# A graph kernel stores its edge records in slot order and loads them into lanes one record at a time

## What is computed

```python
x = x + L0_gnn(layernorm(x), src, dst, ...)      # attention over incoming edges, then a dense layer
x = x + L0_ffn(layernorm(x), ...)                # eight experts, two per node
x = x + L1_gnn(layernorm(x), edge_attr_4, edge_attr_8, (src, dst), ...)
x = x + L1_ffn(layernorm(x), ...)                # two banks of eight experts
```

## Time and profile before

| | us |
|---|---|
| median of 3 runs | 1942.54 (1939.13 to 1943.98) |
| span of the profiled execution | 1941.4 |
| `front`, to the first load of `count_edges` | 322.5 |
| of it from the first to the last scatter's issue | 19.26 to 229.74 |
| `count_edges` | to about 403 |
| attention | to about 709 |
| dense layer, first experts, small network | to about 1272 |
| `messages` | to about 1672 |
| last stage | to 1941.4 |

### The profile page before, as it was taken

One profiled execution on the slowest core, in us unless ns is written; L12 is line 12 of the kernel. 1 busy time (PEld: TensorE's weight loads), 2 busy tenths in 40 slices (PEclk: granted clock), 3 DMA queues, 4 the chain that ended last, 5 costly groups with the idle time before them and its releaser, 6 DMA issues. The chain is left out here.

```text
span 1941.4 us, 31644 instructions
## 1 busy us (share of the span) xinstructions
PE 1611.2 (83%) x9860; PEld 1169.5 (60%) x9860; DVE 958.2 (49%) x1950; ACT 701.1 (36%) x1610; POOL 561.3 (29%) x638
## 2 busy tenths in 40 slices
PE   1132298889999999889999999946999999898994
PEld 0111153568888865555999999934555455654662
DVE  8200023967776657654000000065999999632233
ACT  0000032745555543345222221144555555441331
POOL 6777500020110012125000000044555555123133
PEclk6565598989999999889999999968999999998997
DMA  9600011010103030065766554075555555518985
GB/s 292 240 7 6 18 40 41 1 26 18 23 11 82 10 84 2 1 238 163 284 232 234 197 207 171 9 186 142 159 158 152 146 157 155 190 59 270 354 260 185
DMA packets 131143, 252.87 MB, mean 130 GB/s; under 512 B 35344, under 2 KB 52596, under 8 KB 126572
## 3 DMA queue, kind: packets, MB, share of 16 engines
q1 hardware_dynamic: 91692, 171.81, 26.4%
q0 software_dynamic: 39360, 79.86, 14.7%
HBM read 196.03 MB, written 55.52 MB: 130 GB/s over the span
## 5 line engine op out<-in xcount | busy, mean ns | idle before, releaser
L2065 PE MATMUL acc<-prod,ohy 128*64 128x256 f32 x1056 | 250.7, 387 | 13.7 <-issue 7.5
L2109 ACT ACTIVATE ohy<-oh,RECS 128x64 f32<-128x64 f32 x704 | 186.7, 336 | 160.3 <-PE acc L2065 128.2
L2065 PEld LDWEIGHTS acc<-prod,ohy 128*64 128x64 f32 x1056 | 138.9, 138 | 140.0 <-issue 71.5
L2042 POOL DMA_INDIRECT rows<-up_dram,idx x176 | 167.4, 951 | 151.9 <-DVE prod L2183 107.0
L417 PE MATMUL ps<-FT,Wqkv 128*128 128x512 f32 (+1 forms) x192 | 88.1, 591 | 114.3 <-issue 114.3
L2068 PE MATMUL acc<-prod,ohy 128*64 128x256 f32 x704 | 179.6, 397 | 0.0
L273 POOL DMA_INDIRECT rec_dram<-recs,pos x157 | 161.6, 1029 | 60.2 <-issue 48.9
L1819 DVE TENSOR_SCALAR FT<-y_ps,b2T 128x188 f32<-128x188 f32 x32 | 13.2, 414 | 323.3 <-PE y_ps L1768 323.3
L1756 PE MATMUL hid_ps<-FT,W 128*128 128x188 f32 x1024 | 167.7, 325 | 0.7 <-ACT FT L1793 0.7
L2183 DVE TENSOR_TENSOR prod<-w_ps,rows 128x768 f32<-128x768 f32 x176 | 166.8, 948 | 0.0
L1756 PEld LDWEIGHTS hid_ps<-FT,W 128*128 128x128 f32 x1024 | 165.2, 192 | 0.9 <-issue 0.9
(11 more groups left out here) (389 smaller groups left out, 2725.9 us busy)
## 6 DMA issues: line engine op xcount, KB each, us to landing
W<-in_L_ffn_w SPq DMA_DIRECT2D x16, 4096.0 KB, 16.2
bankW_sp<-in_L_ffn_W_sp SPq DMA_DIRECT2D x2, 4096.0 KB, 24.0
xin<-zeros SPq DMA_DIRECT2D x31, 256.0 KB
h_dram<-h3e SPq DMA_DIRECT2D x22, 256.0 KB
h<-h_dram SPq DMA_DIRECT2D x22, 256.0 KB
QF<-q_dram SPq DMA_DIRECT2D x20, 250.0 KB, 4.2
xin_sp<-zeros SPq DMA_DIRECT2D x17, 256.0 KB
xin_fq<-zeros SPq DMA_DIRECT2D x17, 256.0 KB
```

The source lines that it names most:

```text
L2042: pool.indirect_dma_start(out=rows[:, t, :], out_offset=None, in_=up_dram, in_offset=bass.IndirectOffsetOnAxis(ap=idx[:, par, t:t + 1], ax ...
L2065: upper = lambda m: nc.tensor.matmul(acc[0:HALFB, bank, :].rearrange("p (b c) -> p b c", c=MUL)[:, m:4:3 - m, :], ohs[:, 1 + m, :], pr[:, ...
L2109: last = nc.scalar.activation(ohy[:, t % OHY, i, :], oh[:, par, t, :], ACT.Copy, scale=RECS[:, bass.ds(BATCH * g + t, 1), 4 + i])
```

## The change

Slot s now lies in row s of `rec_dram`. The position is the running sum less one; three VectorE operations per part and two tiles fall away. The loads read row c * 128 + p into lane p, column c, so each lane's neighbouring records lie 8192 bytes apart in memory and each piece is 64 bytes.

```diff
-                slotI, tileI = sb("slotI", [LANES, ECOLS], I32), sb("tileI", [LANES, ECOLS], I32)
...
-                            step(nc.vector.tensor_scalar(slotI[:, mine], posF[:, mine], -1.0, None, ALU.add))
-                            step(nc.vector.tensor_scalar(tileI[:, mine], slotI[:, mine], int(math.log2(LANES)), None, ALU.arith_shift_right))
-                            step(nc.vector.tensor_scalar(slotI[:, mine], slotI[:, mine], LANES - 1, None, ALU.bitwise_and))
-                            step(nc.vector.scalar_tensor_tensor(out=pos[:, mine], in0=slotI[:, mine], scalar=float(ETILES),
-                                                                in1=tileI[:, mine], op0=ALU.mult, op1=ALU.add))
+                            step(nc.vector.tensor_scalar(pos[:, mine], posF[:, mine], -1.0, None, ALU.add))
...
-                            sp.dma_start(RECS[:, c0:c1, :], rec_dram.rearrange("(p c) w -> p c w", p=128)[:, c0:c1, :]
+                            sp.dma_start(RECS[:, c0:c1, :], rec_dram.rearrange("(c p) w -> p c w", p=128)[:, c0:c1, :]
...
-                sp.dma_start(RECS[:], rec_dram.rearrange("(p c) w -> p c w", p=128)).then_inc(loaded, 16)
+                sp.dma_start(RECS[:], rec_dram.rearrange("(c p) w -> p c w", p=128)).then_inc(loaded, 16)
...
-                        sp.dma_start(RECS[:], rec_dram.rearrange("(p c) w -> p c w", p=128)).then_inc(recs_loaded, 16)
+                        sp.dma_start(RECS[:], rec_dram.rearrange("(c p) w -> p c w", p=128)).then_inc(recs_loaded, 16)
```

## The result

The changed kernel takes 1949.2 us (median of 6 runs, 1947.1 to 1952.9), against 1942.4 (6 runs, 1939.1 to 1947.3) of the kernel before beside it: ratio 1.0034, 95% interval 1.0019 to 1.0049. It is slower, by a little over the 0.3% that the prediction called the least to be told from no change. The forecast was 1955, with 1939 to 1999 as its range. The measured change is +6.8 us, where +13 was forecast.

The account below looks back on a forecast made before the run. Bounds: `front`'s slow stretch tied to the scatter count, then waits at the loads' first readers. Terms -1.5 + 2.5 + 0 + 12 = +13 on the 1941.4 span gave 1954.4, so 1955 as median; range 1939 to 1999.

Parts of the forecast that it names:

- first rival: At the record loads, chiefly the `RECS` wait in `messages`: they stay hidden, +1.3 us, 1944, not slower; chance 0.20.
- The price of a piece: In all three strided loads: each 64-byte piece costs 12 ns on its DMA engine, ends 8.4 and 38.7 ns.
- The rival that took QF's price: In `count_edges` and `messages`: a piece costs like QF's 500-byte ones, 38.7 ns, +80 us, 2023; chance 0.15.
- Part 1: Position chain in `front`: three steps fewer give TensorE more work before or inside its slow stretch, -1.5 us (0 to -5.4).
- Part 2: Record load in `count_edges`: VectorE waits 2.5 us longer for the first 48 columns; the remaining columns land hidden.
- Part 3: `RECS_mlp` load of the dense stage: 101 us of cover for 17 us, so it costs nothing.
- Part 4: `RECS` load in `messages`, sharing full DMA engines with GpSimd's gathers: VectorE stands 12.1 us longer, taken as +12.
- the ring of 8: GpSimd's gathers in `messages`: all but two go before VectorE passes tile 5, so the load doesn't put them off.
- the 12 us of idle: Sign in `messages`: line 2148 at about 1310 with some 12 us of idle before it, DMA share near 1 until then.
- the stretch from there to the index keeps its length: In `messages`, the work after the `RECS` wait up to the index needs some 25 us, as before.
- The scatter's pace: Rival in `front`: new write addresses change the scatter, up to 85 us shorter (1857) or 200 us longer; chance 0.06.
- Counting packets: Sign in the profile: over 22000 more packets under 512 bytes per full load.

Follow-up runs that it names:

- after_again: The changed kernel run once more unchanged, for a second profile and set of times: median 1952.9 us against 1940.7, ratio 1.0062 to the kernel before.
- pitch136: Changed kernel with the long four-step position chain and a lane's neighbouring records 8704 bytes apart instead of 8192: ratio 1.0046 to the kernel before.
- loads_only: Changed kernel with the position chain back at four dependent operations per part, so only the strided loads remain: median 1952.1 us, ratio 1.0042 to the kernel before.
- copy_back: Changed kernel, but the dense stage stores its loaded records contiguously to a second buffer that `messages` reads: 1946.0 us, ratio 1.0007 to the kernel before.
- split_load: Changed kernel with the `messages` record load in two, 24 columns early and 152 behind the 16th addition, ahead of the stores: ratio 1.0040 to the kernel before.

## Why the prediction was right, and where it was not

The direction and the range held, the forecast was 6 us high, and the change itself came out at about half of its size. By the table it is worth -0.5 + 2.1 + 0 + 5.7 = +7.3, where the sum was -1.5 + 2.5 + 0 + 12 = +13. The times gave +6.8 in the result and +12.2 beside `after_again` (1952.9 - 1940.7); the 5 us between these two stay open. By its time alone the result lies about as near to the first rival's 1944 as to 1955; the waits decide between them. Of the +5.1 between the two spans only the +2.0 and most of the +6.4 are surely the change's. The -1.7, the +1.6 and the -3.6 come and go in runs of one kernel: the changed kernel's second profile has the end of the front at 323.74, and the kernel before's second has it at 321.90.

**The price of a piece.** Taken as 12 ns, measured by the wall 11.8 and 11.5 in `count_edges`. In the dense stage, after 1.2 MB of x have gone, the queue keeps 109 GB/s, 9.4 ns. In `messages`, where the gathers run beside it, no run isolates it. The choice of 12 was good, in part by luck: it rests on a busy share of 57.1%, and such shares turned out to overstate (117.1% for a queue alone), so 8.4 ns was no measure of the wall. Its other reason, that the 32-byte case was slower by the wall, is the sound one. The rule of the Trainium skill (DMA: Bandwidth & Descriptors, Why small descriptors are slow), 5.9 ns as an estimate that counts only the piece's own 64 bytes, is below all of these. The Trainium skill (same page, Latency and other measured facts) reports down to half rate for rows a large power of two apart. Twice 5.9 is 11.8, and that looked like an answer; at 8704 bytes (`pitch136`), no power of two, the pieces are as slow, so no run here bears it out. The rival that took QF's price is out too.

**Part 1 was mis-sized.** Its steps came as told: first scatter 0.6 us earlier after the same reduction (1.58 instead of 2.20 us), transposes 2.1 us earlier on that count, the same slow pace. What failed is the step from there to the end of `front`: "inside the slow stretch 2.2 us is 1.5 instructions, before it up to three tiles", each worth something at the end. Measured is -0.5 us with a spread of 2. The single profile's -1.7 looked like a confirmation of -1.5 and was for the most part luck; `loads_only` and the kernel before's second profile, with no short chain, show -1.5 as well. Why TensorE's crawl ends when it does, and so what a head start is worth, stays open.

**Part 2 was right.** +2.5 forecast, +2.1 measured, second part hidden. The first keys came at 327.18 rather than 329, as the front ended 1.7 us early and the landing took 6.4 us for 2.3 + 4.6 = 6.9.

**Part 3 was right.** No wait, and none with the load contiguous again.

**Part 4 had the right place and half the cost.** VectorE did stand at the load's landing, as the sum said, but the sum put the landing 29.8 us after the issue and it came after 24.6. Which of its two inputs was too large isn't settled: with 9.4 ns a piece 1408 pieces take 13.2 us and not 16.9, with 11.8 they take 16.6, and then the mistake is to have charged all 10.6 us of the gathers on top, though the two queues' transfers overlap. The step that failed outright is "the ring of 8 lets all but two gathers go before VectorE passes tile 5 ..., so these gathers aren't put off". They are issued early and still arrive late: the wait for `got` grew by 6.1 us, and the 12 us of idle that I looked for at line 2148 came as 1.7. What the stage lost at the first index is 5.7 us, for 12. That the stretch from there to the index keeps its length was right: 25.2 us before and 24.6 after.

**The rivals.** That the loads stay hidden is refuted by the waits for them and by `copy_back`, which takes most of the loss away. The scatter's pace did not change: from the first to the last it is 1.34 us each, before and after.

**Counting packets** was wrong as a sign: I looked for 22000 more under 512 bytes per load; the page of the profile shows 56849 for 35344, some 21500 for all three loads. In `count_edges` 1.44 MB came in 10272 packets, 2.2 records each. A record isn't a packet in this view, so the price has to be reckoned per piece from bytes and time on the wall.

## What to carry to other kernels

A transposing load costs DMA-engine time by the piece, here 9 to 12 ns for 64 bytes on each of 16 engines. Whether it is paid depends on how soon the load is needed and on what else wants the engines then: look for the other queue's transfers too, since most of the wait may show on them and not on the load. A layout that saves three small operations once and is read three times by 22528 pieces needs those reads in stretches with spare DMA time; the two that weren't cost 2 and 6 us against a gain that can't be told from nothing, and both ways out of the larger one (a contiguous copy written in the dense stage; the bulk of the load issued inside the message loop, where VectorE and TensorE are busy all the time), each with the shorter first part, only came back to where the kernel before stood. Before reading a difference of 1 to 2 us out of two profiles, take a second profile of the old kernel.

## What was not expected of the hardware

- A scatter of GpSimd that begins during the scan on VectorE (4.70 us) ends only 0.77 us after the scan's end, where a scatter takes 0.97 us otherwise. What is lost depends on how far into the scan it begins: 3.7 us at 0.78 us, 4.2 us at 0.29. So 0.62 us of head start turned into 0.14.
- A strided load blocks the issuing queue. In `messages` the two small loads behind it took 21.9 us to issue, with the contiguous copy 1.2 us, and with 24 columns strided 5.1 us (`split_load`). Whatever stands behind it in SyncE's order is late too.
- The same load moves 87 GB/s in `count_edges` and 109 GB/s in the dense stage. What makes the difference wasn't tried.
